# Reordering the two-tile step of a fused decoder block: scores, projection, scores, maxima, value products

## What is computed

```python
q = proj(layernorm(x), Wq, 56)                # 16 batches, 16 heads of 8 features
k, v = proj(ctx, Wk, 1500), proj(ctx, Wv, 1500)
scores = einsum('bhqd,bhkd->bhqk', q, k) / sqrt(8) + bias[:, None, None, :]
x = x + einsum('bhqk,bhkd->bhqd', softmax(scores), v) @ Wo.T
# then: softmax router over 32 experts, top 4, capacity 448, per expert
# (silu(xg @ W1[e]) * (xg @ W3[e])) @ W2[e] * weight, plus one shared expert
```

## Time and profile before

| | |
|---|---|
| median of three runs | 589.97 us (588.26 to 594.99) |
| the profiled execution | 591.73 us, span of the trace 590.0 us |
| PE busy | 498.9 us (85%) |
| DVE busy | 383.1 us (65%) |
| ACT busy | 333.8 us (57%) |
| POOL busy | 270.5 us (46%) |
| mean granted TensorE clock | 0.901 of full speed |

### The profile page before, as it was taken

The page is one execution under the profiler, slowest core; times in us unless marked ns, Lnnn a source line. Parts: engine busy times, 40 slices in busy tenths (PEclk is TensorE's granted clock), DMA queues, the critical chain, the costliest instruction groups (busy, mean ns, idle before and its releaser), DMA issues.

```text
span 590.0 us, 17600 instructions
## 1 busy us (share of the span) xinstructions
PE 498.9 (85%) x6656; PEld 312.8 (53%) x6656; DVE 383.1 (65%) x615; ACT 333.8 (57%) x699; POOL 270.5 (46%) x201
## 2 busy tenths in 40 slices
PE   2644988768889999799979999799999887789996
PEld 1224666514556656466646656566666665334442
DVE  6972433579657767477656767477777942588885
ACT  2330165432767777477756777567776684345553
POOL 7895530074672683464570863634440040035540
PEclk9865599956789999899989999799999998599999
DMA  4147184015447547626655347516302210012101
GB/s 135 70 109 149 44 168 123 2 71 143 119 127 149 136 141 133 164 63 169 153 129 157 103 114 168 155 29 152 99 15 87 56 42 14 1 28 54 40 0 32
DMA packets 89117, 56.66 MB, mean 96 GB/s; under 512 B 74910, under 2 KB 80342, under 8 KB 89046
## 3 DMA queue, kind: packets, MB, share of 16 engines
q1 hardware_dynamic: 88390, 55.54, 37.4%
q10 hardware_dynamic: 656, 0.06, 0.1%
HBM read 17.01 MB, written 0.46 MB: 30 GB/s over the span
## 4 chain that ended last, share of the span: by engine, by line
PE 64%; DVE 13%; issue 10%; DMA 7%; ACT 2%; POOL 2%; SPq 1%; ACTq 0%; DVEq 0%; POOLq 0%
PE ps L914 15%; PE ps L797 10%; PE ps L356 8%; DMA qsb<-mrow 6%; PE ps L358 6%; PE ps L357 6%; DVE mx L1523 4%; PE ps L891 3%; PE ps L1018 3%; PE ps L800 3%; PE ps L773 3%; PE ps L807 2%; DVE xn L1305 2%; PE ps L1003 2%; SPq L444 1%
## 5 line engine op out<-in xcount | busy, mean ns | idle before, releaser
L1523 DVE TENSOR_REDUCE mx<-ps 120x2 f32<-120x1000 f32 x192 | 220.8, 1193 | 92.5 <-PE ps L891 92.4
L914 PE MATMUL ps<-qsb,ks 128*125 128x224 f16 x768 | 129.7, 279 | 21.6 <-issue 12.3
L1197 ACT ACTIVATE p<-ps 125x448 f32<-125x448 f32 x256 | 126.2, 540 | 31.5 <-PE ps L914 29.1
L598 POOL TENSOR_TENSOR k<-k,zero 128x500 f16<-128x500 f32 x45 | 45.9, 1020 | 142.9 <-ACT k L1133 142.9
L914 PEld LDWEIGHTS ps<-qsb,ks 128*125 128x125 f16 x768 | 78.8, 140 | 59.5 <-issue 23.7
L1197 ACT ACTIVATE wnat<-ps 125x448 f32<-125x448 f32 x128 | 63.9, 541 | 9.3 <-PE ps L914 9.2
L797 PE MATMUL ps<-p,v 125*27 125x168 f32 x1152 | 67.5, 316 | 0.4 <-DVE v L1429 0.4
L578 POOL TENSOR_TENSOR ch<-ctx,zero 128x1536 f16<-128x1536 f32 x16 | 44.9, 2807 | 23.1 <-issue 19.7
L602 POOL TENSOR_TENSOR k<-k 128x500 f16<-128x500 f32 x45 | 52.8, 1174 | 3.5
L588 POOL TENSOR_TENSOR ch<-ctx,ch 128x1536 f16<-128x1536 f32 x16 | 52.0, 3252 | 3.2 <-DMA ct<-ch 3.1
L1137 ACT ACTIVATE v<-ps 125x512 f32<-125x512 f32 x48 | 28.9, 601 | 43.3 <-PE ps L358 43.1
(11 more groups left out here) (184 smaller groups left out, 897.0 us busy)
## 6 DMA issues: line engine op xcount, KB each, us to landing
ks<-k SPq DMA_DIRECT2D x48, 375.0 KB
ctx<-in_ctx SPq DMA_DIRECT2D x16, 750.0 KB
ks<-in_L_ffn_W SPq DMA_DIRECT2D x48, 64.0 KB, 2.0
qsb<-late SPq DMA_DIRECT2D x32, 56.0 KB, 3.5
ks<-brow SPq DMA_DIRECT2D x32, 46.9 KB
qs<-late SPq DMA_DIRECT2D x8, 168.0 KB, 3.6
qsb<-qd SPq DMA_DIRECT2D x16, 56.0 KB, 2.6
qs<-qd SPq DMA_DIRECT2D x4, 168.0 KB, 3.8
```

The source lines that it names most:

```text
L598: nc.gpsimd.tensor_tensor(k12[:, 0, cols], k32[:, cols], zero[:].rearrange("p a b -> p (a b)").to_broadcast([128, CH]), ALU.add).then_inc( ...
L914: last = mm(stb[half][0:KP, 224 * (g % 2):224 * (g % 2) + 224], ks[c % 3][:, g, KP * s:KP * s + KP], qsb[c % 3][:, HG * g:HG * g + HG].rea ...
L1197: A(p[s % 3][0:KP, 448 * half:448 * half + 448], stb[half][0:KP, 0:448], ACT.Exp, scale=SCALE).then_inc(exp_done, 1)
L1523: V.tensor_reduce(mx[:, h:h + 2, k // 2], mxb[0:120, 2 * pair:2 * pair + 2, 0:CH], axis=AX.X, op=ALU.max).then_inc(mx_read, 1)
```

## The change

- PE's duo becomes: small use, scores of tile 2d, large use, scores of tile 2d+1, max round, two value products. ACT's and DVE's lists follow: ACT copies a small use's result first, then the exponentials of tile 2d, then the projection, then the exponentials of tile 2d+1.
- The order of uses is V0, V1, sel, K0, tr, K1, mt, K2, V2; the small uses sit in duos 2, 3 and 4.
- Maxima are half a batch ahead: duos 0 to 2 do rounds 3 to 5 of the next batch, duos 3 to 5 do rounds 0 to 2 of the batch after it. Three rounds instead of two come ahead of iteration -1.
- There is a fourth probability buffer, which lies over the queries of the self-attention; the exponential of a tile waits for the value products of the tile four before.
- ACT copies the picked heads to a new buffer `heads`, and DVE normalizes from there, with the semaphore `tok_ok` for its result.
- SP issues key stacks first, then queries, then bias rows. POOL splits all three key thirds ahead of the context.
- The gates' matmul has 128 rows: `pairsel` and `gt` are widened, the added rows are zero.

```diff
-MISC = ["V0", "sel", "V1", "tr", "V2", "K0", "mt", "K1", "K2"]
-SMALL = {1: "sel", 2: "tr", 4: "mt"}
-LARGE = ["V0", "V1", "V2", "K0", "K1", "K2"]
-TAIL = {(B - 2, "V0"): "out", (B - 2, "K0"): "norm", (B - 1, "V0"): "logits"}
+MISC = ["V0", "V1", "sel", "K0", "tr", "K1", "mt", "K2", "V2"]
+SMALL = {2: "sel", 3: "tr", 4: "mt"}
+LARGE = ["V0", "V1", "K0", "K1", "K2", "V2"]
+TAIL = {(B - 2, "V0"): "out", (B - 2, "K1"): "norm", (B - 1, "V0"): "logits"}
...
-    return (1, d + 2) if d < 4 else (2, d - 4)
+    return (1, d + 3) if d < 3 else (2, d - 3)
...
+        p.append(qs_rows[:].rearrange("p b h q -> p (b h q)").bitcast(F32)[:, 0:H * S])
...
                     sp.wait_ge(st_done, scores_before(0, i))
+                    key_stacks(i + 2)
+                    load_queries(i + 2)
                     bias_rows(i + 2)
-                    load_queries(i + 2)
-                    key_stacks(i + 2)
...
-                split_keys(i + 3, 0)
+                for j in range(3):
+                    split_keys(i + 3, j)
                 split_first(i + 5)
-                split_keys(i + 3, 1)
-                split_keys(i + 3, 2)
                 split_second(i + 5)
...
             def iteration(r, c):
                 for d in range(ND):
+                    if d in SMALL:
+                        small_use(r, c, SMALL[d])
                     if live(r, c):
                         scores(r, c, 2 * d)
+                    large_use(r, c, LARGE[d])
+                    if live(r, c):
+                        scores(r, c, 2 * d + 1)
+                    off, k = round_of(d)
+                    if live(r, c + off):
+                        max_round(r, c, off, k)
                     for t in (2 * d - 2, 2 * d - 1):
                         if live(r, c if t >= 0 else c - 1):
                             pv_tile(r, c if t >= 0 else c - 1, t % KT)
-                    if live(r, c):
-                        scores(r, c, 2 * d + 1)
-                    if d in SMALL:
-                        small_use(r, c, SMALL[d])
-                    off, k = round_of(d)
-                    if live(r, c + off):
-                        max_round(r, c, off, k)
-                    large_use(r, c, LARGE[d])
...
-            for k in range(2):
+            for k in range(ROUNDS // 2):
                 max_round(0, -2, 2, k)
...
                 if half == 0:
-                    act.wait_ge(pv_done, tile - 2)
-                A(p[s % 3][0:KP, 448 * half:448 * half + 448], stb[half][0:KP, 0:448], ACT.Exp, scale=SCALE
+                    act.wait_ge(pv_done, tile - 3)
+                A(p[s % 4][0:KP, 448 * half:448 * half + 448], stb[half][0:KP, 0:448], ACT.Exp, scale=SCALE
...
+                    use = SMALL.get(d)
+                    if use and used(r, c, use):
+                        act.wait_ge(misc_done, misc_index(r, c, use) + 1)
+                        if use == "sel":
+                            act.wait_ge(tok_ok, 3 * r + c)
+                            A(heads[:], misc[0:S, 0:144], ACT.Copy).then_inc(misc_read, 1)
+                        if use == "tr":
+                            A(attn[:, bass.ds(S * (i - 1), S)], misc[:, 0:S], ACT.Copy).then_inc(misc_read, 1)
+                        if use == "mt":
+                            A(mrow[:], misc[0:H, 0:S], ACT.Copy, scale=1.0 / BIG).then_inc(misc_read, 1)
+                            act.wait_ge(misc_read, misc_index(r, c, use) + 1)
+                            act.dma_start(qsb[(c + 1) % 3][MAXROW:MAXROW + 1], mrow[:]
+                                          ).then_inc(mrow_in[(c + 1) % 3], 16)
                     if live(r, c):
                         exponential(r, c, 2 * d, 0)
                         exponential(r, c, 2 * d, 1)
...
+            V.memset(gt[64:128], 0.0)
             dve.wait_ge(gt_psum, 1)
-            V.tensor_copy(gt, ps[0:64, 5, :].bitcast(F16)[:, 0:T]).then_inc(gt_ok, 1)
+            V.tensor_copy(gt[0:64], ps[0:64, 5, :].bitcast(F16)[:, 0:T]).then_inc(gt_ok, 1)
```

More of the change, by code:

```diff
@@ L161, in build @@
         before = sb("before", [128, 128], F16)
-        pairsel = sb("pairsel", [64, NP, 2, HE], F16)
+        pairsel = sb("pairsel", [128, NP, 2, HE], F16)
         expert_no = sb("expert_no", [128, NE], F32)
@@ L186, in build @@
         attn = sb("attn", [128, T], F32)
-        qs = sb("qs", [SELF_ROWS, B, H, S], F16)
+        qs_rows = sb("qs", [128, B, H, S], F16)
+        qs = qs_rows[0:SELF_ROWS]
         late = sb("late", [128, 2, T], F32)
@@ L216, in build @@
         tok = sb("tok", [128, D], F32)
+        heads = sb("heads", [S, 144], F32)
         flat = lambda t, d, n, o=0: t[:].rearrange("p a b -> p (a b)").bitcast(d)[:, o:o + n]
@@ L297, in build @@
         norm_step = sem("norm_step")
+        tok_ok = sem("tok_ok")
         o_psum = sem("o_psum")
@@ L943, in small_use @@
                 elif use == "tr":
+                    pe.wait_ge(tok_ok, 3 * r + c + 1)
                     tr(misc[:, 0:128], tok[:], ident[:]).then_inc(misc_done, 1)
@@ L1229, in iteration @@
                             take[use[0]](r, c + OFFSET[use[0]], int(use[1]))
+                    if live(r, c):
+                        exponential(r, c, 2 * d + 1, 0)
+                        exponential(r, c, 2 * d + 1, 1)
+                    if d == 0 and live(r, c - 1):
+                        act.wait_ge(pv_done, B + KT * i)
+                        A(osb[:], obank[:, 0:224], ACT.Copy).then_inc(o_read, 1)
                     if d == 1 and isinstance(r, int) and i == B - 1:
@@ L1397, in _ @@
             V.memset(mcol[:], 0.0)
-            V.tensor_tensor(fold[:], ident[0:120, 0:S], ident[0:120, 64:120], ALU.add)
-            V.memset(tok[:], 0.0).then_inc(clear_ok, 1)
+            V.memset(tok[:], 0.0).then_inc(tok_ok, 1)
+            V.tensor_tensor(fold[:], ident[0:120, 0:S], ident[0:120, 64:120], ALU.add).then_inc(clear_ok, 1)
             self_maxima(0)
@@ L1407, in _, with normalize @@
                             ALU.add).then_inc(xb_ok, 1)
-            def normalize(batches):
-                part = misc[0:S, 0:144].rearrange("p (k a e) -> p k a e", k=4, a=4)
+            def normalize(batches, src, done):
+                part = src[0:S, 0:144].rearrange("p (k a e) -> p k a e", k=4, a=4)
                 V.reciprocal(rec[:], part[:, :, :, HD]).then_inc(norm_step, 1)
@@ L1420, in normalize @@
                                 rec[:, 3, :].rearrange("p (a o) -> p a o", o=1).to_broadcast([S, 4, HD]),
-                                ALU.mult).then_inc(misc_read, 1)
+                                ALU.mult).then_inc(done, 1)
             def self_step(r, c):
@@ L1433, in self_step @@
                     dve.wait_ge(misc_done, self_index(r, c, "sel") + 1)
-                    normalize(j - 2)
+                    normalize(j - 2, misc, misc_read)
                 if isinstance(r, int) and j == OUT_STEP:
@@ L1534, in iteration @@
                     if SMALL.get(d) == "sel" and used(r, c, "sel"):
-                        dve.wait_ge(misc_done, misc_index(r, c, "sel") + 1)
-                        normalize(B + i - 1)
+                        dve.wait_ge(misc_read, misc_index(r, c, "sel") + 1)
+                        normalize(B + i - 1, heads, tok_ok)
                     off, k = round_of(d)
```

22 lines of the change are left out of this document (2 added, 20 removed).

## The result

The changed kernel takes 585.31 us (median of 4 runs, 580.99 to 585.92); the kernel before took 591.04 in the same measurement (588.26 to 594.99). The ratio is 0.9887, 95% interval 0.9847 to 0.9926: faster by 1.1%, with an interval of 0.7% to 1.5%. Some executions of any kernel of this document are over 1.5% slower than the fastest of the same kernel; the ratios, and the medians given for runs 6 and 7 and for the kernel before in run 3, leave them out. The profiled execution took 584.87 us with a span of 583.2, against 591.73 and 590.0, so the two traces differ by 6.8 us, where the prediction had 10.0.

What follows compares the result with a forecast made beforehand. A ring through PE and ACT bounds each duo, with waits between batches. Terms -2.3, -5.1, +0.9, +2.5 and -6.0 sum to -10.0, from 591.7 to 581.7; the median before being 1.8 lower, forecast 580.0 us, range 571 to 589.

Steps and rivals of the forecast that it cites:

- ring: Duo's dependence loop through PE and ACT: max round waits for the even exponentials; new duo 3.13 us, max round at 1.89.
- row: DMA of the maxima's row, issued earlier: PE's four waits for it ahead of first scores go, -5.1 us.
- branches: PE's three loop branches back: its list now ends with 64 value-product instructions, 0.3 us more each, +0.9.
- ends: First and last batches: without projections nothing fills ACT's shadow, so the last batches get longer, +2.5 us.
- gates: Experts: with 128 rows the gaps around the gates' matmul fall from 0.29 to 0.19, 30 halves, -6.0 us.
- length of an undisturbed batch: Batches 0 to 12: six duos plus small uses take 20.16 us against 20.34, 0.18 saved each, -2.3.
- 0.1 per duo of unknown neighbours: PE's matmul pairings that no row shows: 0.1 us a duo either way, about 9 us over 90 duos.
- (d): Ring slower because ACT's list is in a tighter order: 0.1 us per duo more, 589, chance 0.14.
- (e): Duo 0.1 us shorter, since scores and projection follow each other without a gap: 571, chance 0.12.
- rival (a): Row's wait stays because its DMA waits for the end of SP's context load: +5.1 us, 585, chance 0.17.
- rival (c): Key stacks land later than 12.0 us into the batch, blocking PE's list; at 1.5 late 601, chance 0.06.
- rival (b): Gates' gaps stay, caused by the changing weights address or the surrounding shapes: +6.0 us, 586, chance 0.08.

Runs made afterwards that it cites:

- run 6: Changed kernel with ACT issuing the maxima row's DMA behind the even tile's two exponentials, not ahead of them: 581.18 us, ratio 0.986.
- Run 7: PE's loop over the batches written out, in the changed kernel (567.46 us, ratio 0.9632) and in the kernel before (576.42 us, ratio 0.9736).
- run 3: Gates' matmul back to 64 rows in the changed kernel (587.69 us, ratio 0.9979); 128 rows alone in the kernel before (589.33 us, ratio 0.9984).
- run 5: Kernel before with only the maxima completed a duo earlier and "mt" in duo 3: 584.46 us against 590.69, ratio 0.99.
- run 1: Changed kernel with SP's old order (bias rows, queries, keys, then the transposes): 577.19 us, ratio to before 0.9786.
- run 2: Changed kernel with SP's order keys, bias rows, queries: 579.69 us, ratio 0.9813.
- Run 4: Changed kernel with GpSimd's two weight-splitting operations each held until DVE finishes a subtraction within SBUF: 580.04 us, ratio 0.982.
- the kernel with all edits: Changed kernel with SP's old order, the row's DMA behind the even exponentials, GpSimd's splits between DVE's subtractions, PE's loop written out: 551.74 us.

## Why the prediction was right, and where its terms were off

The forecast of 580.0 with a range of 571 to 589 and a chance of 0.7 for faster by over 1% stood on a ring, a row, branches, ends and gates. 585.31 lies inside the range, and 1.1% is just over 1%. The ring, the row and the gates' gaps were as described; the gain was 6.8 by the traces and not 10.0, and the terms add up as follows:

| | reckoned | by the traces |
|---|---|---|
| length of an undisturbed batch, thirteen times | -2.3 | -3.9 |
| the row | -5.1 | -6.9 |
| branches, and the duos behind them | +0.9 | +1.7 |
| waits for issue in duo 2 (SP's order) | 0 | +4.0 |
| the rest of batches 0 to 12 | 0 | +0.6 |
| ends | +2.5 | +0.2 |
| gates | -6.0 | -2.5 |
| sum | -10.0 | -6.8 |

Three terms gave 5.7 us more than reckoned, and the others took 8.9 back. That the total came as near as 3.2 us is in part luck.

- **The duo: right.** 3.13 reckoned, 3.14 measured, and the projection, moved into ACT's shadow, costs nothing. "sel" costs 0.53 (duo 1, 3.66) and "tr" 0.17 (duo 2, 3.30), as said. "mt" costs 0.03 (duo 3, 3.16) and not 0.21, for a reason not followed up. ACT's issue costs 0.53 rather than 0.44; run 6 took just this away. A batch is 20.04, not 20.16. The 0.1 per duo of unknown neighbours, which made the widest bound (rivals (d) and (e)), was nought.
- **The row: right, and worth more.** No wait is left, and run 5 confirms it alone; rival (a) is out. The last duos of batches 0, 2, 5 and 8 had 5.6 us too much, and the slow first duo of batch 1 1.3 more.
- **The step that failed** is the sentence on the row, "Next late would be the key stacks", with rival (c)'s condition as the only price of SP's new order. What was late was PE's own list. The new order of three short issues let the transposes follow the bias rows directly, and PE, waiting for nothing it computes on, lost 4.0 us in duo 2 and more elsewhere. Runs 1 and 2 show the order as the cause, and 5.2 to 7.1 us as its price by the traces. The prediction had costed SP's order at nought and asked only whether the data come in time. Run 7 shows that the order alone is not enough: with PE's loop written out and SP's new order the waits are gone. How the DMAs hold up PE's issue in duo 2 is not shown. That PE stands at the same two places of its list (in run 6 at a third too) points to the fetch of its instructions, as at the branches; but no packet of that queue was late by the trace. By the Trainium skill ("DMA: Bandwidth & Descriptors", on queues and completion order) a completion is written only after every earlier write of the same SDMA engine. That would fit a packet that is in and not yet reported; no run here shows it.
- **Branches:** +0.9 reckoned. The last duos at the branches grew by 2.4 and the duos behind them shrank by 0.6. Of the 2.4, 1.7 went with SP's old order in run 1 and 0.6 with that of run 2. What is left is near the 0.9, but no run tests the reason that the prediction gave, 64 instructions in place of a projection. The prediction also held that the row's waits hidden in these pauses bring nothing back; run 5 has 0.5 to 1.0 us a branch less, so that was too strict.
- **Gates: right mechanism, half the size.** The gaps were 0.29 for 64 rows and are 0.19 for 128, which run 3 shows in both directions; rival (b) is out. The rule of "TensorE: Matmul & The Clock Gate" in the Trainium skill, the same time for a small contraction, holds here for the matmul itself (0.36 with 64 rows, 0.35 with 128), not for its distance from its neighbours. Why a change of the rows costs 0.1 on either side is not shown. But the term was 6.0 and gave 2.5. The prediction did write that if DVE became the bound "half of the gain would be left", and excluded it by DVE's mean of 1.73 us of work in 2.10. The mean was no argument: one of DVE's three operations gets 0.48 longer when it meets GpSimd. Run 4 took the meeting away and the whole term appeared, 6.1.
- **Ends:** +2.5 reckoned, +0.2 measured: batch 13 takes 19.57 (19.33 before), not 20.16, and from the start of batch 14 to the last value products are 37.3 us (36.6 before), not 38.0; against that, batch 0 starts 0.35 earlier, and from the last value products to the first gates there is 0.4 less, so the hop through ACT costs nothing that shows.

## What to carry to other kernels

When a change reorders DMA issues, ask not only whether each transfer still lands in time, but what now stands next to what, and look for new "issue" waits on an engine that has all its operands. When an engine stage gets faster, lay out the timeline of every engine for one period at the new length: an engine that is idle a fifth of the time can still have its one critical operation fall upon another engine's. Settle an order of issues by trying it with nothing else changed: here it took back as much as the whole rest had gained. And a pause at a branch back is worth measuring first: here three of them cost more than twice what the whole reordering of the duo, the maxima and the gates gained.

## What was unexpected of the hardware

- A branch back over a body of three batches (about 1,000 matmuls and as many weight loads) costs PE 5 to 6 us: 2.6 to 5.3 us without issue, until 1.6 to 1.9 us behind the last packet of instructions, and then a duo at a granted clock of 0.61 (at the first branch of the changed kernel). Written out, the kernel with all edits is 17.2 us faster.
- PE can stand for 0.4 to 1.9 us with its operands there, mostly at the same two places of its list in four kernels, because of the order in which another engine issues DMAs; written out, the same list with the same order has none of it.
- A DMA issue on ACT costs 0.53 us of the ring when it stands ahead of an exponential, and nothing when it stands behind one, since it then runs beside it.
- The same 55.54 MB keep the DMA queue busy 38.0% (queries last), 39.8% (keys last) or 45.6% (bias rows last) of the span, only by which transfer is issued directly ahead of the transposes.
- DVE's subtraction within SBUF takes 1.10 instead of 0.62 us, and GpSimd's 1.18 instead of 0.92, when the two meet; DVE's products that read PSUM and SBUF kept their 0.61 beside GpSimd.
